# A ring of neighbour pixels laid out over all 128 partitions instead of 112 in a row

## The reference

```python
ux, uy, uxx, uxy, uyy = derivs(u)          # 3x3 Sobel filters, and Sobel of Sobel: up to 5x5, all clipped to +-10
g2 = ux*ux + uy*uy
K = clip((uxx*uyy - uxy*uxy) / ((1+g2)**2 + EPS), -5, 5)
H = clip(((1+uy*uy)*uxx - 2*ux*uy*uxy + (1+ux*ux)*uyy) / (2*sqrt(1+g2+EPS)**3 + EPS), -5, 5)
u = u + DT*clip(alpha*K + beta*H, -1, 1)   # ten times; after each step the image's outer pixels are copied from the inner ones
x1 = 0.7*u + 0.3*x
out = conv(relu(conv(x1, w1) + b1), w2) + b2 + x1
```

## Time and profile before

| what | value |
|---|---|
| median of 3 runs | 40639.29 us (40620.17 to 40643.75) |
| the profiled execution's own time | 40599.69 us |
| its span, first to last instruction | 40597.9 us |
| PE / DVE / ACT / POOL busy | 86% / 84% / 82% / 50% of the span |
| mean share of the 16 DMA engines on SyncE's queue | 56.8% |
| mean granted TensorE clock | 0.971 |

### The profile page before, as it was taken

How to read it: one execution, slowest core, us unless ns; L and a number is a source line. 1 busy time by engine, 2 the same in 40 slices (tenths; PEclk the granted TensorE clock), 3 DMA queues, 4 the chain that set the end, 5 groups by cost and what they waited for, 6 DMA issues and landing times. The chain is left out here.

```text
span 40597.9 us, 445411 instructions
## 1 busy us (share of the span) xinstructions
PE 34779.5 (86%) x120896; PEld 22578.0 (56%) x120896; DVE 34223.0 (84%) x31730; ACT 33168.8 (82%) x33722; POOL 20444.4 (50%) x7685
## 2 busy tenths in 40 slices
PE   5888888888888888888888888888888888888999
PEld 3555555555555555555555555555555555554444
DVE  8999999999999999999999999999999999994111
ACT  5888889888888889888888889888888889885333
POOL 3555555555555555555555555555555555551000
PEclk9999999999999999999999999999999999999999
DMA  7555556555555555555555556555555556554333
GB/s 181 79 78 79 79 75 76 77 79 79 79 79 79 79 74 76 77 79 79 78 78 79 79 74 77 77 79 78 79 79 79 78 76 76 77 78 88 99 99 97
DMA packets 2728323, 3335.51 MB, mean 82 GB/s; under 512 B 2236356, under 2 KB 2236484, under 8 KB 2422212
## 3 DMA queue, kind: packets, MB, share of 16 engines
q1 hardware_dynamic: 2727364, 3324.78, 56.8%
HBM read 626.33 MB, written 301.47 MB: 23 GB/s over the span
## 5 line engine op out<-in xcount | busy, mean ns | idle before, releaser
L645 PE MATMUL tame_slot<-tame_split,tame_M 128*128 128x512 f32 x51200 | 15359.2, 422 | 5684.4 <-DVE tame_ux L516 3252.1
L645 PEld LDWEIGHTS tame_slot<-tame_split,tame_M 128*128 128x128 f32 x51200 | 9234.4, 192 | 11664.9 <-DVE tame_cross L516 3060.2
L645 PE MATMUL tame_slot<-tame_halo,tame_M 112*128 112x512 f32 x51200 | 14449.7, 404 | 0.0
L357 POOL TENSOR_TENSOR tame_split<-tame_U,tame_split 128x1024 fp32r<-128x1024 f32 x2560 | 6230.8, 2434 | 12957.1 <-ACT tame_split L392 12957.1
L645 PEld LDWEIGHTS tame_slot<-tame_halo,tame_M 112*128 112x128 f32 x51200 | 9855.4, 192 | 2544.4
L369 POOL TENSOR_TENSOR tame_ux<-tame_ux,tame_cross 128x1024 f32<-128x1024 f32 x2560 | 8063.4, 3150 | 436.3 <-POOL tame_ux L363 436.3
L363 POOL TENSOR_TENSOR tame_ux<-tame_ux,tame_uy 128x1024 f32<-128x1024 f32 x2560 | 6151.2, 2403 | 2695.9 <-DVE tame_uy L516 2695.9
L655 PE MATMUL tame_slot<-tame_uxy,tame_unit 128*128 128x512 f32 x10240 | 4962.0, 607 | 7.2 <-DVE tame_slot L539 7.2
L432 ACT ACTIVATE tame_slope<-tame_slope 128x2048 f32<-128x2048 f32 x2560 | 4894.9, 1912 | 0.0
L427 ACT ACTIVATE tame_slope<-tame_slope 128x1024 f32<-128x1024 f32 x2560 | 2717.5, 1062 | 2153.1 <-issue 2151.1
L558 DVE TENSOR_TENSOR tame_uyy<-tame_slot,tame_slope 128x1024 f32<-128x1024 f32 x2560 | 3135.7, 1225 | 1201.1 <-PE tame_slot L655 1189.8
(11 more groups left out here) (58 smaller groups left out, 36779.3 us busy)
## 6 DMA issues: line engine op xcount, KB each, us to landing
tame_halo<-tame_split SPq DMA_DIRECT2D x2560, 520.0 KB
tame_halo<-tame_split SPq DMA_DIRECT2D x2560, 260.0 KB
tame_halo<-tame_split SPq DMA_DIRECT2D x5120, 65.0 KB
xin<-mixed SPq DMA_DIRECT2D x672, 319.0 KB, 4.3
tame_U<-in_x SPq DMA_DIRECT2D x256, 512.0 KB, 3.7
tame_stage<-in_x SPq DMA_DIRECT2D x128, 1024.0 KB, 8.4
mixed<-tame_stage SPq DMA_DIRECT2D x1024, 128.0 KB, 2.5
out<-res SPq DMA_DIRECT2D x672, 192.0 KB
```

Source lines behind the costliest of these rows:

```text
L357: nc.gpsimd.tensor_tensor(split_rows(c, 1), half_rows(c), split_rows(c, 0).bitcast(F32), ALU.subtract).then_inc(lo_ready, 2)
L645: last = nc.tensor.matmul(ps[name][:, b * BANK:(b + 1) * BANK], M[0:lanes, matrix, :], rows(c, part)[:, b * y:(b + 1) * y, :], start=(n < ...
```

## The change

The ring lies over all 128 partitions. A RING entry has two more numbers, the first partition of its lot in `halo` and the distance between its partitions: left at 0, 4, 8, ...; right at 1, 5, 9, ...; top at 2, 10, 18, ...; bottom at 6, 14, 22, ...; the corners at 3, 7, 11 and 15, each 32 apart. These fill 112 partitions; the 16 others (19, 23, 27, 31 and so on) hold no ring pixel. The DMAs have the same sources, sizes and order as before, and write to every fourth, eighth or thirty-second partition. The matmuls on `halo` have 128 rows instead of 112; the rows of M for the 16 empty partitions are zero, and DVE clears both `halo` tiles once at the start, for which SyncE's first exchange waits (`ring_zeroed`).

```diff
     return [
-        (left, PC // 2, 2 * PR, -1), (right, PC // 2, 2 * PR, 1),
-        (top, 1, 2 * PC, -WIDE), (bottom, 1, 2 * PC, WIDE),
-        (top + left, PC // 2, 4, -WIDE - 1), (top + right, PC // 2, 4, -WIDE + 1),
-        (bottom + left, PC // 2, 4, WIDE - 1), (bottom + right, PC // 2, 4, WIDE + 1),
+        (left, PC // 2, 2 * PR, -1, 0, 4), (right, PC // 2, 2 * PR, 1, 1, 4),
+        (top, 1, 2 * PC, -WIDE, 2, 8), (bottom, 1, 2 * PC, WIDE, 6, 8),
+        (top + left, PC // 2, 4, -WIDE - 1, 3, 32), (top + right, PC // 2, 4, -WIDE + 1, 7, 32),
+        (bottom + left, PC // 2, 4, WIDE - 1, 11, 32), (bottom + right, PC // 2, 4, WIDE + 1, 15, 32),
     ]
...
-        halo = [sb(f"halo{j}", [HALO, 2, RUN], F32R) for j in range(2)]
+        halo = [sb(f"halo{j}", [P, 2, RUN], F32R) for j in range(2)]
...
             def exchange(i, j, part):
-                at = 0
-                for m, (first, step, n, shift) in enumerate(RING):
-                    if m // (len(RING) // 2) == part:
-                        sp.dma_start(halo[j][at:at + n, :, :].bitcast(F32),
-                                     split[i][first:first + (n - 1) * step + 1:step, :,
-                                              BEFORE + shift:BEFORE + shift + RUN].bitcast(F32)).then_inc(halo_in[i], 16)
-                    at += n
+                for first, step, n, shift, to, apart in RING[part * 4:part * 4 + 4]:
+                    sp.dma_start(halo[j][to:to + (n - 1) * apart + 1:apart, :, :].bitcast(F32),
+                                 split[i][first:first + (n - 1) * step + 1:step, :,
+                                          BEFORE + shift:BEFORE + shift + RUN].bitcast(F32)).then_inc(halo_in[i], 16)
...
             sp.wait_ge(stencils_rounded, 1)
+            sp.wait_ge(ring_zeroed, 1)
             sp.wait_ge(lo_ready, 4)
...
             nc.vector.memset(split[SLOTS - 1][:, :, :].bitcast(F32), 0.0).then_inc(zeroed, 1)
+            nc.vector.memset(halo[0][:, :, :].bitcast(F32), 0.0)
+            nc.vector.memset(halo[1][:, :, :].bitcast(F32), 0.0).then_inc(ring_zeroed, 1)
...
-                for matrix, lanes, rows in ((f, P, split_rows), (len(ORDER) + f, HALO, halo_rows)):
+                for matrix, lanes, rows in ((f, P, split_rows), (len(ORDER) + f, P, halo_rows)):
```

More of the change, by code:

```diff
@@ L65, in ring_runs @@
     return [
-        (left, PC // 2, 2 * PR, -1), (right, PC // 2, 2 * PR, 1),
-        (top, 1, 2 * PC, -WIDE), (bottom, 1, 2 * PC, WIDE),
-        (top + left, PC // 2, 4, -WIDE - 1), (top + right, PC // 2, 4, -WIDE + 1),
-        (bottom + left, PC // 2, 4, WIDE - 1), (bottom + right, PC // 2, 4, WIDE + 1),
+        (left, PC // 2, 2 * PR, -1, 0, 4), (right, PC // 2, 2 * PR, 1, 1, 4),
+        (top, 1, 2 * PC, -WIDE, 2, 8), (bottom, 1, 2 * PC, WIDE, 6, 8),
+        (top + left, PC // 2, 4, -WIDE - 1, 3, 32), (top + right, PC // 2, 4, -WIDE + 1, 7, 32),
+        (bottom + left, PC // 2, 4, WIDE - 1, 11, 32), (bottom + right, PC // 2, 4, WIDE + 1, 15, 32),
     ]
 RING = ring_runs()
-HALO = sum(n for _, _, n, _ in RING)
 def stencil_matrices():
@@ L84, in stencil_matrices @@
     inside = [pixel[k] for k in range(P)]
-    ring = []
-    for first, step, n, shift in RING:
+    ring = [None] * P
+    for first, step, n, shift, to, apart in RING:
         down = (shift + WIDE + 1) // WIDE - 1
         across = shift - down * WIDE
-        ring += [(pixel[k][0] + down * PR, pixel[k][1] + across * PC) for k in range(first, first + n * step, step)]
+        for m in range(n):
+            r, c = pixel[first + m * step]
+            ring[to + m * apart] = (r + down * PR, c + across * PC)
     for f, name in enumerate(ORDER):
@@ L93, in stencil_matrices @@
         for m, pixels in ((f, inside), (len(ORDER) + f, ring)):
-            for k, (sr, sc) in enumerate(pixels):
+            for k, source in enumerate(pixels):
+                if source is None:
+                    continue
+                sr, sc = source
                 for o, (r, c) in enumerate(inside):
@@ L162, in curvature_flow @@
         zeroed = sem("zeroed")
+        ring_zeroed = sem("ring_zeroed")
         param_step = sem("param_step")
```

## The result

The changed kernel's median is 39638.33 us in 4 runs (39631.13 to 39640.43), against 40630.49 us in 4 runs of the kernel before (40620.17 to 40643.75). The ratio is 0.9755, with a 95% interval from 0.9738 to 0.9772: 2.45% faster, 992 us. Forecast were 39770 us and 868 us less. The profiled execution took 39640.43 us with a span of 39638.6 us, 959 us under the span before.

What follows compares the result with a forecast made beforehand. DVE was taken to bound the middle steps, with its closing-step blends waiting for edge copies behind the ring; 813 (blends) + 50 (other waits) + 5 (start) = 868 us less, about 39770 us, range 39590 to 40260.

Steps and rivals of the forecast that it cites:

- The bound: DVE sets the middle steps' pace; in closing steps 127 blends wait 1153.6 us for edge copies queued behind the ring.
- The sign that was named for the queue: In SyncE's queue, the edge row would be issued about 5 us sooner after the edge columns.
- part 1: Large ring transfers: left and right at twice the pace, saving 4.5 us; top and bottom gain nothing, at most 3.2 us.
- part 2: Corner transfers, 7.6 us at 35 GB/s: factor 2 saves 3.8 us, between 0 and 5.4.
- part 3: DVE's blends: each long wait shrinks by D, not under 2.03 us; 813 us saved, 896 with all at the floor.
- D: How much sooner an edge row behind both ring lots comes: 4.5 + 3.8 = 8.3 us, between 0 and 15.0.
- part 4: Waits of ACT for edge copies and PE for the ring: 50 us saved, between 0 and 142.
- part 5: Start: clearing delays the first exchange 3 us, which is then D shorter; 5 us saved.
- part 6: Ring matmuls with 128 rows instead of 112: no added time taken, 18 ns each as the other end.
- No effect of the target: The second rival: source or shifted runs set the transfers' pace, not the target; 40642 us, no change, chance 0.11.
- dearer matmuls: Rival: 128-row ring matmuls on the path cost 18 ns more each, 184 us; 40826 us, slower, chance 0.05.
- partial gain: Rival: only part of the ring's pace is gained; with D = 3, 384 us saved, 40255 us, chance 0.19.

Runs made afterwards that it cites:

- run with other sources: Changed kernel with top and bottom reading every eighth partition from 0 instead of 16 in a row: 39618.28 us, ratio 0.9755 to the kernel before.
- run with a step of two: Kernel before with 128 rows, corners spread 8 apart, and left, right, top and bottom on every second partition: 39887.72 us, ratio 0.982.
- run with the corners alone: Kernel before with 128 rows and clearing; corners spread 8 apart from partition 96, large transfers still in a row: 40150.48 us, ratio 0.9885.
- ring in a row: Changed kernel with the ring back on partitions 0 to 111, keeping 128 matmul rows and clearing: 40573.36 us against 40614.92, ratio 0.999.
- ACT's scaling moved: Changed kernel with ACT's scaling of x by 0.3 issued before the same period's logarithm: 39314.81 us against the kernel before's 40609.61, ratio 0.9683.

## Why the prediction was right

**The bound.** Right. The middle period kept its rest of 0.42 us, and the gain lies in the blends, 840 us of 959. The sign that was named for the queue came too: the edge row was issued 10.8 us after its edge columns, and is now 4.3 us after them, 6.5 us sooner where about 5 were forecast. That all 256 blends would wait about 2 us held for 225.

**Left and right (part 1).** I took twice the pace and 4.5 us. It was three times (135 to 410 GB/s), the other end of what I had allowed: 7.9 us became 2.6, a saving of 5.3. The reason for factor 2, that both sides stay in SBUF, was wrong; SBUF to SBUF reached the loads' pace, 410 against 414 GB/s.

**Top and bottom (part 1).** Next to no gain, as taken: 5.1 us became 4.6. The run with other sources (116 to 198 GB/s) supports the reason given, the 16 partitions in a row that they are read from; but the run with a step of two reached 196 GB/s from these same sources, so it is not the whole reason.

**Corners (part 2).** Factor 2 and 3.8 us were taken; 36 to 72 GB/s and 7.9 to 3.6 us were measured.

**The blends (part 3).** 813 us forecast, 840 measured, with ACT's 2.03 us as the floor that I had named. The sum of both savings as one D was too simple, as the run with the corners alone shows (2.4 us a blend for 4.3 us of transfer). It did no harm, since with both lots faster nearly every wait reaches the floor. For the same reason the good agreement is in part luck: the floor holds the gain at 896 us at most, so the time hardly tests the paces that were taken. The windows do, and there left and right were off by a factor of 1.5.

**Other waits (part 4).** I took 50 of at most 142 us. The whole 142 left the list of waits, but what they were worth is read from DVE's own rests. These two fell, before (first two lines) and after:

```profile
L516 DVE SCALAR_TENSOR_TENSOR tame_slope<-tame_ux,tame_uy 128x1024 f32<-128x1024 f32 x2560 | 3112.0, 1216 | 17.0 <-ACT tame_uy L409 16.8
L516 DVE SCALAR_TENSOR_TENSOR tame_cross<-tame_cross,tame_slot 128x1024 f32<-128x1024 f32 x2560 | 3108.6, 1214 | 46.9 <-issue 46.9
```

```profile
L522 DVE SCALAR_TENSOR_TENSOR tame_slope<-tame_ux,tame_uy 128x1024 f32<-128x1024 f32 x2560 | 3111.4, 1215 | 1.3 <-ACT tame_uy L413 1.3
L522 DVE SCALAR_TENSOR_TENSOR tame_cross<-tame_cross,tame_slot 128x1024 f32<-128x1024 f32 x2560 | 3107.5, 1214 | 0.0
```

That is 63 us, a little more than the 50. That they hung on those waits of ACT and PE is inferred: both sorts are gone together in the run with the corners alone as well, and both are still there with the ring in a row. The rest of the 959 us was in no term: DVE's update of U from `tame_ux` took 3689.4 us in all instead of 3721.0, and its rests before the product with `tame_cross` fell from 412.2 to 381.6 us, 18.5 of that at the start.

**The start (part 5).** PE's first matmul begins at 415.6 instead of 421.9, 6 us sooner; 5 were forecast, but of two errors that cancel. The exchange began at 402.2 instead of 396.88, 5.3 us later where 3 were taken (the scan before it ended 2.3 us later in this run), and it took 13.5 us to the first matmul instead of 25.0, 11.5 less where D was 8.3.

**Matmuls with 128 rows (part 6).** 0, as taken: the group's mean is 404 ns as before, and the run with the row count alone was not slower. The groups' means of 422 and 404 ns had not come from the row counts, since 404 is now the mean of matmuls with 128 rows.

**The rivals.** No effect of the target is ruled out by the changed kernel and the run with the ring in a row, which have the same sources; dearer matmuls by the latter; and partial gain by the changed kernel's time itself. One ground for the second rival was misread: transfers to 32 and to 16 partitions did not have one pace. The window of 12 us at 119 GB/s held both kinds, and apart they are 135 and 110. That the sources count too, which I had kept as a doubt, turned out true for top and bottom in the changed layout.

## What to carry to other kernels

If DMA engines are all busy and move a fraction of what they move in the best transfer of the same trace (here 135 against 414 GB/s, at a share of 1.04 and 1.03), look at which partitions they work on at the same time, on the reading and the writing side. Where a matmul sums over the partitions, their order is free, since the weights can be permuted on the host; here the wider layout cost the matmuls nothing that was measured (a mean of 404 ns with 112 rows and with 128). And a transfer that nobody seems to wait for can still cost time through the small copies that stand behind it in its queue, here 1153.6 us of blends' waits; once it is shortened, name the next floor and try to lower it, because then its speed can count again, as it did here: with ACT's scaling moved, 95 blends waited for an edge copy instead of 30.

## What was not expected of the hardware

- A step of 2 between target partitions left the pace of left and right at 131 GB/s, a step of 4 gave 410. The same partitions in two transfers of 16 instead of one of 32 fell to 253.
- A copy from SBUF to SBUF reached 410 GB/s, as fast as the loads from memory (414).
- The mean granted clock of TensorE rose from 0.971 to 0.982 with the shorter waits, and to 0.986 with the scaling moved. In the middle stretches it was 1.00 before and after. In the closing step of the earlier trace rows it was 0.74 where PE was busy 0.87 of 10 us, and 1.00 where it was busy 8.67; what that was worth was not measured apart. The kernel before, around the first blend:

```profile
2540.00:2550.00 10.00, 8.67 (x35) 6.25 (x34) 10.00 (x10) 9.06 (x9) 5.67 (x3) 1.00 0.49 68
...
2560.00:2570.00 10.00, 0.87 (x4) 0.37 (x2) 2.99 (x3) 4.50 (x5) 0.50 (x1) 0.74 0.15 29
```
